# A two-block graph network on one core: chunks turned by PE and the identity, or by transposing DMAs

## What is computed

```python
h = relu(layernorm(x))
x = x + L0(h)       # log_softmax(sage(relu(sage(h, W1, b1)), W2, b2))
h = relu(layernorm(x))
x = x + L1(h)       # conv(128->256), relu, conv(256->256), relu, linear, relu, linear
# sage(h):  concat[h, segment_sum(h[src], dst) / max(deg, 1)] @ W + b
# conv(h):  (segment_sum(h[src], dst) / max(deg, 1)) @ Wl.T + bl + h @ Wr.T
```

## Time and profile before

| | us |
|---|---|
| median of 3 runs | 587.8 (587.75 to 589.28) |
| the profiled execution, time | 587.56 |
| its span, first to last instruction | 585.7 |
| PE busy | 544.2 (93%) |
| DVE busy | 225.0 |
| ACT busy | 202.9 |
| DMA bytes | 29.47 MB, 50 GB/s over the span |

### The profile page before, as it was taken

One profiled execution on the slowest core, in us unless ns is written; L12 is line 12 of the kernel. 1 busy time (PEld: TensorE's weight loads), 2 busy tenths in 40 slices (PEclk: granted clock), 3 DMA queues, 4 the chain that ended last, 5 costly groups with the idle time before them and its releaser, 6 DMA issues.

```text
span 585.7 us, 9420 instructions
## 1 busy us (share of the span) xinstructions
PE 544.2 (93%) x3078; PEld 291.5 (50%) x3078; DVE 225.0 (38%) x500; ACT 202.9 (35%) x368; POOL 24.7 (4%) x36
## 2 busy tenths in 40 slices
PE   1367999999999999999999999999999999999996
PEld 0244655555554654445455555644545445454555
DVE  6899959577775217667411111110000001010001
ACT  1688858567664304455422222200000010100011
POOL 4410000000000000110100000000000000000000
PEclk9997999999999999999999999999999999999999
DMA  3800103010010124333121111232011212111011
GB/s 94 196 1 1 38 1 117 2 36 17 17 35 17 24 70 112 90 90 77 39 76 53 52 52 39 67 117 52 19 35 39 49 35 52 35 35 52 17 32 30
DMA packets 31372, 29.47 MB, mean 50 GB/s; under 512 B 4894, under 2 KB 30879, under 8 KB 31215
## 3 DMA queue, kind: packets, MB, share of 16 engines
q1 hardware_dynamic: 29622, 27.91, 17.6%
q10 hardware_dynamic: 1561, 0.84, 0.6%
q0 software_dynamic: 160, 0.33, 0.2%
HBM read 19.68 MB, written 9.39 MB: 50 GB/s over the span
## 4 chain that ended last, share of the span: by engine, by line
PE 87%; DVE 5%; ACT 3%; DMA 2%; issue 2%; POOL 1%; ACTq 0%; SPq 0%; DVEq 0%; POOLq 0%
PE ps L1036 54%; PE ps L1053 22%; PE ps L990 6%; PE ps L1308 2%; DVE hs_b L493 2%; PE ps L1046 1%; PE ps L1270 1%; DMA hs_b<-self_d 1%; DMA adj<-key_d,adj 1%; ACT adj L1490 1%; POOL adj L1375 1%; PE ps L1242 1%; DVE adj L1426 1%; DMA adj<-in_dst_dram 0%; ACT adj L844 0%
## 5 line engine op out<-in xcount | busy, mean ns | idle before, releaser
L1036 PE MATMUL ps<-adj,hs_b 125*128 (+2 forms) x1050 | 203.6, 351 | 0.0
L1036 PE MATMUL ps<-adj,hs_a 125*128 (+2 forms) x700 | 158.5, 353 | 0.0
L1036 PEld LDWEIGHTS ps<-adj,hs_b 125*128 125x128 f16 x1050 | 96.3, 97 | 103.9 <-issue 6.6
L493 DVE TENSOR_TENSOR hs_b<-iota,hs_b 128x1024 f16<-128x1024 f16 x150 | 95.4, 685 | 27.9 <-PE ps L990 26.9
L844 ACT ACTIVATE adj<-ps 125x500 f32 (+2 forms) x150 | 80.0, 544 | 22.8 <-PE ps L990 16.6
L990 PE MATMUL ps<-hs_b 128*128 128x125 f16 x625 | 68.5, 233 | 20.7 <-DVE hs_b L493 13.1
L990 PEld LDWEIGHTS ps<-hs_b 128*128 128x128 f16 x625 | 46.5, 103 | 65.7 <-DVE hs_b L493 34.4
L1036 PEld LDWEIGHTS ps<-adj,hs_a 125*128 125x128 f16 x700 | 58.5, 98 | 38.8 <-issue 5.4
L975 ACT ACTIVATE actT<-ps,col 128x500 f32<-128x500 f32 (+1 forms) x14 | 8.9, 633 | 148.0 <-PE ps L1053 148.0
L791 DVE TENSOR_TENSOR hs_a<-ps,hs_a 125x512 f32<-125x512 f32 (+1 forms) x7 | 4.4, 634 | 128.9 <-PE ps L1308 128.9
L1053 PE MATMUL ps<-aggT,wts 128*128 128x500 f32 (+1 forms) x112 | 44.6, 540 | 0.4 <-ACT aggT L957 0.4
(11 more groups left out here) (150 smaller groups left out, 356.4 us busy)
## 6 DMA issues: line engine op xcount, KB each, us to landing
invc<-inv_d SPq DMA_DIRECT2D x24, 250.0 KB, 3.3
h_d<-actT SPq DMA_DIRECT2D x6, 500.0 KB, 3.1
wts<-h_d SPq DMA_DIRECT2D x6, 500.0 KB, 4.0
self_d<-hs_b SPq DMA_DIRECT2D x6, 250.0 KB, 2.1
hs_b<-self_d SPq DMA_DIRECT2D x6, 250.0 KB, 3.5
hs_b<-in_x_dram SPq DMA_DIRECT2D x6, 250.0 KB
x_d<-hs_b SPq DMA_DIRECT2D x6, 250.0 KB
hs_a<-x_d SPq DMA_DIRECT2D x6, 250.0 KB
```

Of the source, the lines that this page charges most:

```text
L493: last = nc.vector.tensor_tensor(onehots[slot], iota2.unsqueeze(1).to_broadcast(shape), keys[:, ds(g * 4, 4), :].unsqueeze(2).to_broadcast ...
L1036: last = nc.tensor.matmul(acc[:, 0:n], hs[:, ds(s * (2 * w) + part * w + h * 128, 128)], adj[0:P, ds(c * (S * C) + s * n, n)], start=(isin ...
```

## The change

For full chunks four of the turns leave PE.

- *Own rows*, phases 1 and 3 (`own1`, `own3`, chunks 0 to 5): the rows (high and low half) are stored to DRAM (`hs_d1` in five pieces, `hs_d3` chunk by chunk in phase 2); SP loads each half with a transposing DMA (512 rows x 128, float16) into a buffer, and DVE adds the two (`own_sum`). ACT no longer evicts them.
- *z*, phase 1 (`turn1`, chunks 0 to 5): ACT and DVE write the halves untransposed in float16 (`z_out`, `z_low`), SP stores them to `z_d`, waits for the landing, and loads each 125 nodes with a transposing DMA (256 rows x 128) into `hs_b`.
- *The hidden features*, phase 3 (`turn3`, chunks 0 to 4): the same by way of `h16_d`, with two stores of 256 KB and four transposing DMAs (512 rows x 128) per chunk.
- In phase 1 DVE's order is new: `self_out` and `z_low` of chunk c-2 after group 9, `own_sum` after group 15, in place of `low` after group 3 and `self_out` after group 18. On SP the load of the next inverse degrees, then the turns of the next chunk's own rows, stand ahead of the stores.
- In phase 3 the sums alternate between banks 1 and 2, and PE waits for the eviction of the chunk before the last.

The short chunk, and chunk 5 in phase 3, keep PE's turns. The slow path's semaphores are merged. The core of the diff (its lines of the slow path and of phase 4's waits left out):

```diff
+        PT = 128
+        z16 = [zT[:, :].bitcast(F16)[:, k * 4 * PT:(k + 1) * 4 * PT] for k in range(2)]
+        turned1 = [hs_b[:, (20 + 2 * k) * 2 * D:(22 + 2 * k) * 2 * D] for k in range(2)]
+        turned3 = [hs_b[:, (20 + k) * 2 * H:(21 + k) * 2 * H] for k in range(2)]
+        zboth = zT[:, :].bitcast(F16)
+        h16 = [v.bitcast(F16).rearrange("p (m t n) -> p m t n", m=2, n=PT) for v in (zT[:, :], wts[:, 512:1024])]
+        ND = NFULL - 1
...
+            def turn_own(ph, c, hd, into):
+                for k in range(2):
+                    sp.dma_start_transpose(into[k], hd[ds(c * C, 512), k * D:(k + 1) * D]).then_inc(sem(f"p{ph}_hT"), 16)
...
+            def next_inv(c, nxt):
                 sp.wait_ge(sem("p1_agg_out"), c + 1)
-                if nxt is not None:
-                    load_inv("p1_", c + 1, nxt)
-                if not slow and isinstance(c, int) and c == 0:
-                    store_weights()
+                load_inv("p1_", c + 1, nxt)
+            def self_rows(c, full):
                 sp.wait_ge(sem("p1_self"), c + 1)
                 sp.dma_start(self_d[:, ds(c * C, width(full))], selfT[:, 0:width(full)]).then_inc(sem("p1_self_out"), 16)
-            each(step1)
+            def z_rows(c):
+                sp.wait_ge(sem("p1_zlo"), c + 1)
+                sp.dma_start(z_d[ds(c * 256, 256), :].rearrange("(k f) n -> f k n", k=2),
+                             zboth.rearrange("p (k n) -> p k n", k=2)).then_inc(sem("p1_z_out"), 16)
+                sp.wait_ge(sem("p1_z_out"), 16 * c + 16)
+                for t in range(4):
+                    sp.dma_start_transpose(hs_b[:, ds(c * (4 * 2 * D) + t * 2 * D, 2 * D)],
+                                           z_d[ds(c * 256, 256), t * PT:(t + 1) * PT]).then_inc(sem("p1_zin"), 16)
+            def step1(c):
+                next_inv(c, True)
+                sp.wait_ge(sem("p1_h0T"), c + 1)
+                turn_own(1, c + 1, hs_d1, turned1)
+                if isinstance(c, int) and c == 0:
+                    store_weights()
+                else:
+                    self_rows(c - 1, True)
+                    z_rows(c - 1)
+            def slow1(c, full, nxt):
+                if nxt is not None:
+                    next_inv(c, nxt)
+                self_rows(c, full)
+            if slow:
+                each(slow1)
+            else:
+                step1(0)
+                with sp.Fori(1, NFULL - 1) as c:
+                    step1(c)
+                for c in range(NFULL - 2, NFULL):
+                    self_rows(c, True)
+                    z_rows(c)
+                    if c < NFULL - 1:
+                        next_inv(NFULL - 1, False)
+                self_rows(NFULL, False)
...
+                if not slow and not (isinstance(c, int) and c == 0):
+                    sp.wait_ge(sem("p2_low"), c)
+                    sp.dma_start(hs_d3[ds((c - 1) * C, C), :].rearrange("(t p) f -> p t f", p=P),
+                                 ha[:, ds((c - 1) * (4 * 2 * D), 4 * 2 * D)].rearrange("p (t f) -> p t f", f=2 * D)).then_inc(
+                        sem("p2_rows"), 16)
...
+                sp.wait_ge(sem("p2_rows"), 16 * NFULL)
+                turn_own(3, 0, hs_d3, turned3)
...
+            def turn_rows(c):
+                sp.wait_ge(sem("p3_st"), 32 * c + 32)
+                for t in range(4):
+                    sp.dma_start_transpose(hs_b[:, ds(c * (4 * 2 * H) + t * 2 * H, 2 * H)],
+                                           h16_d[ds(c * 512, 512), t * PT:(t + 1) * PT]).then_inc(sem("p3_in"), 16)
             def step3(c, full, nxt):
                 if nxt is not None:
                     sp.wait_ge(sem("p3_agg_out"), c + 1)
                     load_inv("p3_", c + 1, nxt)
+                if not slow and nxt:
+                    if isinstance(c, int) and c == 0:
+                        sp.wait_ge(sem("p2_rows"), 16 * NCH)
+                    sp.wait_ge(sem("p3_ownT"), c + 1)
+                    turn_own(3, c + 1, hs_d3, turned3)
+                if not slow and full and not (isinstance(c, int) and c == 0):
+                    turn_rows(c - 1)
                 n = width(full)
                 sp.wait_ge(sem("p3_relu"), 2 * c + 2)
                 sp.dma_start(h3_d[:, :, ds(c * C, n)],
                              actT.rearrange("p (m n) -> p m n", m=2)[:, :, 0:n]).then_inc(sem("p3_h3_out"), 16)
+                if not slow and full and not (isinstance(c, int) and c == ND):
+                    for k, half in enumerate(("p3_hi", "p3_lo")):
+                        sp.wait_ge(sem(half), c + 1)
+                        sp.dma_start(h16_d[ds(c * 512 + k * 256, 256), :].rearrange("(m f) n -> f m n", m=2),
+                                     h16[k].rearrange("p m t n -> p m (t n)")).then_inc(sem("p3_st"), 16)
...
+        def rows_out(sp, a, b):
+            for j in range(a, b):
+                sp.wait_ge(sem("n_low"), j + 1)
+                sp.dma_start(hs_d1[j * PIECE * P:(j + 1) * PIECE * P, :].rearrange("(t p) f -> p t f", p=P),
+                             tiles(ha, 2 * D)[:, j * PIECE:(j + 1) * PIECE, :]).then_inc(sem("h0_rows"), 16)
...
+            def own_sum(ph, c, parts):
+                dve.wait_ge(sem(f"p{ph}_hT"), 32 * c + 32)
+                wait_past(dve, "p1_h1" if ph == 1 else "p3_h3", 2 * c)
+                nc.vector.tensor_tensor(aggT[:, C:2 * C], parts[0][:, 0:C], parts[1][:, 0:C], ALU.add).then_inc(
+                    sem("p1_h0T" if ph == 1 else "p3_ownT"), 1)
+            def z_low(c):
+                dve.wait_ge(sem("p1_zT"), c + 1)
+                by_tile = lambda v: v.rearrange("p (t n) -> p t n", n=PT)[:, :, 0:P]
+                nc.vector.scalar_tensor_tensor(by_tile(z16[1]), bank(6, C).rearrange("p (t n) -> p t n", n=P), zs, by_tile(z16[0]),
+                                               ALU.mult, ALU.subtract).then_inc(sem("p1_zlo"), 1)
...
+                    dve.wait_ge(sem("inv_out"), 16)
+                    nc.vector.memset(zboth.rearrange("p (t n) -> p t n", n=PT)[:, :, P:PT], 0.0)
+                    own_sum(1, 0, turned1)
                     weights_dve(dve, 0)
                     build_c(c + 1, nxt, 0, 1)
                     weights_dve(dve, 1)
-                    build_c(c + 1, nxt, 1, 5)
+                    build_c(c + 1, nxt, 1, 4)
                 else:
-                    low(c - 2, True)
                     if nxt is not None:
-                        build_c(c + 1, nxt, 0, 5)
-                self_out(c - 1, True)
+                        build_c(c + 1, nxt, 0, 2)
+                    if c is not NFULL:
+                        self_out(c - 2, True)
+                        z_low(c - 2)
+                    if nxt is not None:
+                        build_c(c + 1, nxt, 2, 4)
+                if c is not NFULL:
+                    own_sum(1, c, turned1)
                 if nxt is not None:
-                    build_c(c + 1, nxt, 5, 7)
+                    build_c(c + 1, nxt, 4, 7)
+                if not nxt:
+                    self_out(c - 1, True)
+                    z_low(c - 1)
...
+                if full and not slow and not last_full:
+                    dve.wait_ge(sem("p3_hi"), c + 1)
+                    wait_past(dve, "p3_st", 32 * c)
+                    for m in range(2):
+                        last = nc.vector.tensor_tensor(h16[1][:, m, :, 0:P],
+                                                       actT[:, m * C:(m + 1) * C].rearrange("p (t n) -> p t n", n=P),
+                                                       h16[0][:, m, :, 0:P], ALU.subtract)
+                    last.then_inc(sem("p3_lo"), 1)
+                    return
...
+                by_dma = full and not slow
+                if by_dma:
+                    own_sum(3, c, turned3)
+                if by_dma and not first and not (isinstance(c, int) and c == 1):
                     low3(c - 1, True)
-            step3(0, True, first=True)
-            step3(1, True)
-            with dve.Fori(2, NFULL) as c:
-                step3(c, True)
-            step3(NFULL, False)
+                agg_out3()
+                if not first and not (by_dma and not (isinstance(c, int) and c == 1)):
+                    low3(c - 1, True)
...
+                    wait_past(act, "p1_zin", 64 * c)
+                    nc.scalar.activation(z16[0].rearrange("p (t n) -> p t n", n=PT)[:, :, 0:P],
+                                         bank(6, n).rearrange("p (t n) -> p t n", n=P), ACT.Identity, scale=zs).then_inc(
+                        sem("p1_zT"), 1)
+                    return
...
+                    pe.wait_ge(sem("p1_zlo"), NFULL)
...
+                    wait_past(pe, "p1_zlo", c)
...
-                own1(c - 1, True)
...
-                turn1(c - 1, True)
...
+                            wait_past(pe, f"p{ph}_agg_out", c - 1 if ph == 3 else len(aggs) * (c - 1) + at // S + 1)
...
+                with pe.Fori(1, NFULL // 2) as h:
```

(59 more changed lines are left out.)

149 lines of the change are left out of this document (91 added, 58 removed).

## The result

The changed kernel is slower: 594.43 us median of 4 runs (592.49 to 596.33), against 587.81 (587.75 to 589.28) for the kernel before, a ratio of 1.0106 with the interval 1.0065 to 1.0148. The forecast was 578.4. The profiled execution took 592.49, span 590.7, so 5.0 us more than before by the span.

A forecast was written before the change was run, and what follows sets the result against it. PE was taken to bound the kernel (busy 544.2 of 585.7 us). Phase 3 7.7 + phase 1 borders 2.8 - chunk 1 0.85 - phase 3's start 0.5 = 9.2 us off 587.56: 578.4, range 574.5 to 597.

The forecast's parts named there:

- Phase 3, steady chunks: Borders in phase 3: PE saves 1.37 us before each of chunks 2 to 5 and 1.79 before short chunk 6.
- Phase 1, chunks 2 to 5: Four phase 1 borders, each about 0.7 us shorter because DVE's `low` leaves the stretch: 2.8 us gained.
- rival (b): Gain partly given back: `z_out` or phase 3's first layer waits, or DVE passes stick out; 583 us, chance 0.17.
- End of phase 1: Chunk 6 and phase 1's end: sum eviction and `z_low` on DVE leave PE no gain, 0.
- Chunk 1: Phase 1, chunk 1: clearing of pads and sum of halves delay DVE, already late there; 0.85 us lost.
- 2 us of air by my 3.3 + 0.35: Phase 1, chunk 1: DVE's sum stands behind a turn on SP's queue, claimed to have 2 us to spare.
- Start of phase 3: Before phase 3's first dense layer: store, turns, sum and eviction against PE, a dead heat; 0.5 us wait, bounds 0 to 3.3.
- POOL's clearing: At the start POOL clears one more tile; with POOL busy 4%, claimed to cost nothing.
- (c): Nothing changes, within 0.3% or 1.8 us: turns one behind another at some 2.5 us each; chance 0.06.
- (a): Turns run one behind another and become the bound, in phase 3 from 2.3 us a turn; 613 us, chance 0.19.
- DVE's sum waiting for `hs_b<-hs_d`: Sign in the profile after: DVE's sum of halves waits for a turn's load out of DRAM, meaning turns are the bound.

The follow-up runs named there:

- e5: Changed kernel with chunk 0's own rows turned by PE again in phases 1 and 3, and phase 3's first inverse degrees loaded ahead of the turns: 579.81 us.
- e8: Phase 1 entirely as in the kernel before, phases 2 and 3 as in e5, without POOL's clearing of zT: 581.22 us.
- e6: e5 with the 125-partition stores of both layers' rows split into 112 + 13 and without POOL's clearing of zT: 580.17 us.
- e3: Changed kernel with phase 2's stores of the second layer's rows split into partitions 0 to 111 and 112 to 124: 589.76 us.
- e1: Changed kernel with each store of h0's rows split into partitions 0 to 111 and 112 to 124: 592.55 us.
- e4: Changed kernel with the splits of e1 and e3, no POOL clearing of zT, and phase 3's first inverse degrees loaded ahead of the turns: 584.36 us.
- e9: e6 with nine idle DVE passes ahead of DVE's work on the weights in chunk 1, DMAs unchanged: 586.37 us.
- e7: Changed kernel with chunk 0's own rows turned by PE again in phase 1 alone, phase 3's start as changed: 587.51 us.
- e2: Changed kernel with each store of h0's rows made two DMAs of 2 and 3 tiles, both of all 125 partitions: 592.98 us in one run.

## Why the prediction was wrong, and where it was right

The sum forecast -9.2; the trace shows +5.0. By its own steps:

- **Phase 3, steady chunks: right.** Forecast 1.37 us at each of four borders and 1.79 before the short chunk. In e5, by the table, 1.38, 1.36, 1.36, 1.37 and 1.78. The two banks hide the eviction, and six turns of 128 KB in 13.92 us are no bound.
- **Phase 1, chunks 2 to 5: right in e5** (2.72 us, from 100.30 to 97.58 between the layers of chunks 0 and 4; forecast 2.8), **1.91 in the changed kernel**. The border itself is shorter as worked out, though PE now waits 0.49 for ACT and 0.25 for the sum's eviction there. The shortfall sits between the layers of chunks 1 and 2 (0.23), where the store of z took 1.38 us to issue (0.39 in the others) and PE waited 0.40 for ACT behind a late `z_out`. ACT waited 8.4 us for z's turns over these chunks, 3.4 at most, nearly all without effect: rival (b)'s mechanism, at a fraction of its price.
- **End of phase 1:** forecast 0. The short chunk lost some 0.45 (PE waits 0.92 for the sum's eviction, behind `z_low` on DVE), and by phase 2's first turn the net since chunk 4's layer was 0 in the changed kernel; in e5, where the load that phase 2's first turn waits for (as it did before) was hardly earlier (issued at 213.46, before 213.62), 1.24 of the gain was lost by then (175.09 to 219.38 against 176.55 to 219.60). That, not a dearer turn, is why phase 1 nets so little in e8's comparison.
- **Chunk 1: the step that failed.** "2 us of air by my 3.3 + 0.35" took the turn's landing from a row (2.71 measured, a safe bound) and gives no price for the store; at the start of phase 3 the prediction takes a store's from the earlier trace rows, 2.1 us for 250 KB. That store, `self_d`, has 128 partitions, and the rows' stores have 125: 8.83 us to land, 2.86 to issue two. Forecast loss 0.85, measured 6.77: a longer stop, and 1.3 us of half clock (from resuming to the layer 3.78 us, in e5 2.48).
- **Start of phase 3: the same step failed again.** Store 5.31 in place of 2.1; issue of the turns 1.22 each in place of 0.35; the inverse degrees, forecast at "about 295.0, still ahead of the eviction's turn", landed at 304.99 as the last of all. PE waited 4.36 us where 0.5 was booked and 3.3 was the bound, and the layer started 3.66 us late (booked: 0.5, less the 0.44 of `own3`); 3.07 us of half clock, which the prediction doesn't mention at all, came on top.
- **POOL's clearing, "so nothing":** 0.6 us up to the first counting. The 4% of busy time lies at the very start, where the chain runs through DVE. Whether any of it reaches the end isn't shown: e6, without the clearing, is no faster than e5.

The misses add up: 0.8 at the start (the clearing, and what scatter there is from trace to trace), 5.9 in chunk 1, 0.9 in phase 1's borders, 3.6 and 3.1 at phase 3's start, -0.1 behind it, together 14.2, which is 9.2 + 5.0.

That 594.43 lies inside the outermost range, up to 597, is luck: that end was drawn for rivals (b) and (c) and the mild part of (a), and what took the time was none of them.

Of the rivals, (a) is refuted: turns take 2.3 to 3.0 us to land but overlap, SP issues the next 1.2 us after the last, and a chunk of phase 3 has PE busy throughout. With that the Trainium skill's 1309 ns per 128x128 block ("VectorE: DVE Perf Modes", The three transpose paths) is no price for a stream of turns here: 24 blocks would be 31 us, and they fit into 13.92. What the Trainium skill says in "Advanced Engine Details and Errata", X-Bar Transpose (TRN2), that they are as fast as plain DMAs, is near for the landings (3.0 us for 128 KB turned, 3.4 for the 250 KB load of inverse degrees) and not so for the issue (1.22 against 0.35). The time that came about lies between (b) and (a), by neither: a gain that was real, and two fixed losses where a phase begins and nothing is in flight yet. The signal that the prediction named for rival (a), DVE's sum waiting for `hs_b<-hs_d`, did show (4.67 us), but from the store ahead of the turn.

## What to carry to other kernels

A step moved to DMA pays off in the steady loop, where its latency has cover, and must be priced apart for the first chunk, where store, landing, issue and load stand one behind another; leaving the first chunk on the old engine, and a load ahead of the turns (e5), cost 0.44 us of PE in each of two phases and was worth 14.6 (594.43 - 579.81), 14.3 by the ratios. Take the price of a store from a row with the same number of partitions, not only the same bytes, and price the issue of each DMA by its kind, with what is queued behind it. A forecast stop of several us of PE should carry a second term for the half clock that follows it.

## What the runs showed of the hardware

- **Partitions of a store.** Two stores of 312.5 KB from 125 partitions: 0.37 and 2.45 us to issue, in DRAM 9.3 us after the first issue began, at a DMA share of 0.35. Split 112 + 13: four issues in 2.43 us, in DRAM after 4.9 us, at a share up to 0.77. 250 KB: 5.3 against 2.7 us. The issue time doesn't follow from the shape: three stores before them, of the same 312.5 KB, cost 0.27 to 0.30 us each.
- **A transposing DMA** costs SP 1.22 us to issue (2.43 for two, 5.0 for four), where a plain one takes 0.35; in the changed kernel it lands 2.3 us (64 KB) to 3.0 us (128 KB) after issue.
- **PE's clock after a stop.** PE idle, the lowest granted clock, and the duration of the next dense layer in the timeline:

| place | PE idle | clock | layer |
|---|---|---|---|
| e5, chunk 1 | 1.19 | 1.00 | 3.60 |
| e3, start of phase 3 | 1.82 | 1.00 | 3.59 |
| e1, chunk 1 | 3.33 | 0.50 | 3.60 |
| e4, chunk 1 | 3.92 | 0.50 | 6.05 |
| e9, chunk 1 (made by DVE) | 4.13 | 0.50 | 5.74 |
| after, start of phase 3 | 4.36 | 0.50 | 6.42 |
| e7, start of phase 3 | 4.74 | 0.50 | 6.03 |
| after, chunk 1 | 7.07 | 0.50 | 3.60 |
| e2, chunk 1 | 7.09 | 0.50 | 3.60 |
| e3, chunk 1 | 7.46 | 0.50 | 5.94 |

Where the layer took 3.60 after a clock of 0.50, the spell had ended before it began; in e3's chunk 1 it reached into the stretch from 88 to 90 (0.58). A long stop isn't the only thing that goes before a spell: in the kernel before the clock is 0.54 from 44 to 48, where PE is busy for 1.42 of 4 us in short pieces. The price differs from run to run, and the kernels with a long stop scatter over 2.3 to 7.5 us where e5 scatters over 1.1.
